# One attention block with its feed-forward part on one core: scales from norms, values by DMA transposes, and score tiles taken in pairs

## The reference

```python
c_kv = x @ w_dkv;  c_q = x @ w_dq
k_r = rope(x @ w_kr)                    # one for all heads
k = concat(k_r, c_kv @ w_uk);  q = concat(rope(c_q @ w_qr), c_q @ w_uq)
v = c_kv @ w_uv
attn = softmax(q @ k.T / sqrt(192));  out = (attn @ v) @ w_o
x = layernorm(x + out)
x = layernorm(x + (silu(x @ w1q.T) * (x @ w3q.T)) @ w2q.T)   # ternary weights
```

## Time and profile before

| | |
|---|---|
| median of three runs | 1019.66 us |
| profiled execution | 1020.77 us |
| its span | 1019.1 us |
| granted TensorE clock, mean | 0.974 of full |
| set-up | 0 to about 47 us |
| stage before the loop, batch 0 | about 47 to 112 us |
| loop, batch 0 | about 112 to 458 us |
| output, norms, feed-forward, batch 0 | about 458 to 527 us |
| loop, batch 1 | about 593 to 940 us |

### The profile page before, as it was taken

How to read it: one execution, slowest core, us unless ns; L and a number is a source line. 1 busy time by engine, 2 the same in 40 slices (tenths; PEclk the granted TensorE clock), 3 DMA queues, 4 the chain that set the end, 5 groups by cost and what they waited for, 6 DMA issues and landing times.

```text
span 1019.1 us, 17708 instructions
## 1 busy us (share of the span) xinstructions
PE 891.6 (87%) x5114; PEld 502.5 (49%) x5114; DVE 681.3 (67%) x1060; ACT 695.9 (68%) x1116; POOL 596.0 (58%) x401
## 2 busy tenths in 40 slices
PE   7888869998999999989889876999999999998985
PEld 3556534444444444448775642444444444444874
DVE  1877747777777777764458674777777777776455
ACT  2733668888888888881333466888888888887132
POOL 0008856767777767772341874776777776777134
PEclk9998979999999999999999897999999999999998
DMA  9734698887778877884510669897878877889301
GB/s 252 231 141 104 148 221 153 149 152 149 145 148 154 153 148 145 146 157 134 180 36 12 132 161 192 148 152 150 153 143 150 154 149 145 151 146 157 120 1 41
DMA packets 420800, 145.34 MB, mean 143 GB/s; under 512 B 405820, under 2 KB 413840, under 8 KB 419728
## 3 DMA queue, kind: packets, MB, share of 16 engines
q1 hardware_dynamic: 419584, 136.88, 67.5%
q10 hardware_dynamic: 592, 5.77, 1.4%
q0 software_dynamic: 576, 2.10, 0.6%
HBM read 23.85 MB, written 7.60 MB: 31 GB/s over the span
## 4 chain that ended last, share of the span: by engine, by line
PE 28%; ACT 25%; issue 20%; DVE 11%; POOL 9%; DMA 3%; ACTq 2%; SPq 1%; POOLq 0%; DVEq 0%
ACT probs L566 11%; ACT P_parts L451 8%; POOL P_parts L398 6%; PE Sb L1103 6%; DVE nmax L825 5%; PE Oa L1132 4%; ACT PT_hi L451 3%; PE Sa L1103 3%; DMA PT_dma<-P_parts 2%; ACT rden_row L451 2%; POOL g_lo L427 1%; DVE qmul L804 1%; PE Sa L1156 1%; PE Sb L1156 1%; DVE Q_parts L795 1%
## 5 line engine op out<-in xcount | busy, mean ns | idle before, releaser
L398 POOL TENSOR_TENSOR P_parts<-probs,P_parts 128x768 f16<-128x768 f32 x256 | 420.8, 1645 | 210.2 <-ACT P_parts L451 210.2
L451 ACT ACTIVATE P_parts<-probs 128x768 f16<-128x768 f32 x256 | 214.3, 838 | 17.0 <-DMA PT_dma<-P_parts 17.0
L566 ACT ACTIVATE probs<-Sa,nmax,limits 128x1024 f32<-128x1024 f32 x128 | 154.0, 1203 | 90.3 <-DVE nmax L828 90.1
L825 DVE TENSOR_REDUCE nmax<-Sb 128x1 f32<-128x1024 f32 x128 | 156.5, 1223 | 55.9 <-PE Sb L1103 55.7
L1103 PE MATMUL Sb<-K_hi,Q_parts 128*128 128x512 f16 x512 | 155.1, 385 | 43.6 <-ACT probs L566 42.8
L1103 PE MATMUL Sa<-K_hi,Q_parts 128*128 128x512 f16 x512 | 156.3, 388 | 34.8 <-ACT probs L566 34.7
L825 DVE TENSOR_REDUCE nmax<-Sa 128x1 f32<-128x1024 f32 x128 | 154.9, 1210 | 29.1 <-PE Sa L1103 29.1
L566 ACT ACTIVATE probs<-Sb,nmax,limits 128x1024 f32<-128x1024 f32 x128 | 154.3, 1205 | 1.5 <-DVE nmax L828 1.5
L1132 PE MATMUL Oa<-PT_dma,V_hi 128*64 128x512 f16 x768 | 132.4, 385 | 0.0
L1103 PEld LDWEIGHTS Sa<-K_hi,Q_parts 128*128 (+1 forms) x512 | 40.1, 99 | 118.7 <-issue 61.2
L371 POOL TENSOR_TENSOR turned<-qmul 128x1024 f32<-128x1024 f32 x16 | 40.1, 2528 | 93.5 <-DVE qmul L804 93.4
(11 more groups left out here) (300 smaller groups left out, 1536.6 us busy)
## 6 DMA issues: line engine op xcount, KB each, us to landing
Q_parts<-turned_parts SPq DMA_DIRECT2D x64, 128.0 KB, 2.4
TT<-ternary SPq DMA_DIRECT2D x2, 2304.0 KB, 9.7
Q_parts<-Q_parts SPq DMA_DIRECT2D x16, 256.0 KB, 2.9
PT_dma<-P_parts SPq DMA_TRANSPOSE x256, 3.6
ternary<-tern ACTq DMA_DIRECT2D x1, 2304.0 KB, 8.2
wo<-in_L_attn_w_o_dram SPq DMA_DIRECT2D x4, 512.0 KB, 8.6
xq<-in_L_attn_x_dram SPq DMA_DIRECT2D x2, 1024.0 KB, 12.1
wq_low<-Wq_lo ACTq DMA_DIRECT2D x1, 2048.0 KB, 12.7
```

Of the source, the lines that this page charges most:

```text
L398: nc.gpsimd.tensor_tensor(P_parts[:, n % DEEP, 1, :], probs[n % DEEP][:, KP * P:S], P_parts[:, n % DEEP, 0, :], ALU.subtract).then_inc(par ...
L451: return nc.scalar.activation(o, i, ACT.Copy, scale=scale)
L566: nc.scalar.activation(probs[n % DEEP], SS[n % 2][:, :], ACT.Exp, bias=nmax[:, n % 4:n % 4 + 1], scale=score_down, accum_out=den[:, n // 8 ...
L825: nc.vector.tensor_reduce(nmax[:, n % 4:n % 4 + 1], SS[n % 2][:, :], AX.X, ALU.max, negate=True).then_inc(row_max, 1)
```

## The change

Four things are changed together.

The scales of the fp16 parts are no longer taken from the computed keys and queries but bounded from norms: the largest sum of squares of a row of x (eight squares with accumulation on ScalarE), the largest entries of the key and query weights and the sum of squares of w_dq, with a square root by a power on GpSimd. They are known before the keys are cut, so K_hi and K_lo are cut straight from PSUM; the latent half by ScalarE and VectorE, the rotated half by GpSimd's sums. The query latent is scaled when it is cut, and later steps on queries carry no scale.

The values are no longer transposed by TensorE; SP issues two DMA transposes of the latent halves of K_hi and K_lo.

In the loop two tiles are taken at a time: TensorE computes two score tiles, then values, then the transposes of both; ScalarE makes two exponents, then the eviction PT_hi, then two casts; VectorE takes two maxima, then PT_lo, and now copies the row of sums. VectorE makes one normalising product, and GpSimd casts its high part.

The stores of the low weights pass from ScalarE's to SP's queue, and the low part of the rotary weights from VectorE to GpSimd.

```diff
 # scalar: before the loop
-                act_.wait_ge(proj_in, b * 208 + 208)
+                act_.wait_ge(w_in, b * 160 + 160)
...
+                act_.wait_ge(y_ready, b * 2 + Y0)
+                for t in range(QT):
+                    nc.scalar.activation(qmul[:, t // 4, t % 4 * D:t % 4 * D + D], xq[:, t, :], ACT.Square,
+                                         accum_out=x_sums[:, t:t + 1]).then_inc(x_sq, 1)
...
+                scaled(K_hi[64:128, :], Sa[64:128, :], k_up[64:128]).then_inc(k_lat_hi, 1)
+                scaled(cq_hi[:, :], Sb[:, :], cq_up).then_inc(cq_hid, 1)
...
 # scalar: the loop
-                    for n in range(TILES):
...
-                            exponent(t0 + n + 1, n + 1)
-                        part_high(t0 + n, n, None if first and n < DEEP else 16 * (t0 // DEEP + n // DEEP))
-                        if n % 2:
-                            transposed_high(t0 + n, n)
-                        if n in (3, 11) and not (first and n == 3):
-                            row_out(pair * 2 + (n // 8) - 1)
+                    for n in range(0, TILES, 2):
+                        ahead = not (last and n == TILES - 2)
+                        if ahead:
+                            exponent(t0 + n + 2, n + 2)
+                        if ahead:
+                            exponent(t0 + n + 3, n + 3)
+                        transposed_high(t0 + n + 1, n + 1)
+                        if ahead:
+                            for m in (n + 2, n + 3):
+                                part_high(t0 + m, m, None if first and m < DEEP else 16 * (t0 // DEEP + m // DEEP))
 # vector: before the loop
+                nc.vector.tensor_reduce(kv_most, wkv[:, :, :].rearrange("p c m -> p (c m)"), AX.X, ALU.max,
+                                        apply_absolute_value=True).then_inc(w_max, 1)
...
+                nc.vector.tensor_reduce(x_most, x_sums[:, :], AX.X, ALU.max).then_inc(x_max, 1)
+                dve.wait_ge(x_row, b + 1)
+                nc.vector.tensor_reduce(sums[0:1, 7:8], Oa[0:1, 0:P], AX.X, ALU.max).then_inc(x_top, 1)
+                dve.wait_ge(sums_ps, b + 1)
...
+                dve.wait_ge(lim_pow, b + 1)
...
+                for out_rows, in_rows, o, table in (...):
+                    nc.vector.scalar_tensor_tensor(o[out_rows, :], Sa[in_rows, :], k_up[in_rows], table[in_rows, :],
+                                                   ALU.mult, ALU.mult).then_inc(k_mul, 1)
+                nc.vector.scalar_tensor_tensor(K_lo[64:128, :], Sa[64:128, :], k_up[64:128], K_hi[64:128, :], ALU.mult,
+                                               ALU.subtract).then_inc(k_lat_lo, 1)
-                nc.vector.tensor_reduce(k_sum, Kf[:, :], AX.X, ALU.max, apply_absolute_value=True).then_inc(k_step, 1)
-                nc.vector.tensor_reduce(q_most[:, 0:1], cq_hi[:, :].bitcast(F), AX.X, ALU.max, ...)
-                nc.vector.tensor_reduce(q_most[:, 1:2], cq_s[:, :].bitcast(F), AX.X, ALU.max, ...)
...
 # vector: the loop
+                def row_out(group):
+                    dve.wait_ge(row_ps, group + 1)
+                    dve.wait_ge(out_ready, group + 1)
+                    nc.vector.tensor_copy(rden_row[:, :], Ob[:, :]).then_inc(row_ready, 1)
...
-                        if not (last and n >= TILES - 2):
+                        if not (last and n == TILES - 2):
                             maximum(t0 + n + 2, n + 2)
-                        if n % 2:
-                            transposed_low(pair * (TILES // 2) + n // 2, n)
+                            maximum(t0 + n + 3, n + 3)
+                        transposed_low(pair * (TILES // 2) + n // 2, n + 1)
+                        if n % 8 == 2 and not (first and n == 2):
+                            row_out(pair * 2 + n // 8 - 1)
 # gpsimd
+                pool.wait_ge(lim_step, b * LSTEPS + 5)
+                nc.gpsimd.tensor_tensor(pow_of, pow_in, minus_half[:, 0:2], ALU.pow).then_inc(lim_pow, 1)
+                pool.wait_ge(k_mul, b * 3 + 3)
+                nc.gpsimd.tensor_tensor(kmul[0:32, :], kmul[0:32, :], kturn[0:32, :], ALU.subtract).then_inc(k_rot, 1)
+                nc.gpsimd.tensor_tensor(kmul[32:64, :], kmul[32:64, :], kturn[32:64, :], ALU.add).then_inc(k_rot, 1)
...
+                nc.gpsimd.tensor_tensor(K_lo[0:64, :], kmul[0:64, :], K_hi[0:64, :], ALU.subtract).then_inc(k_rot_lo, 1)
...
+                    nc.gpsimd.tensor_copy(O_parts[:, pair_row, cols], QO[:, pair_row + 1, cols]).then_inc(out_hi, 1)
 # sync
+                sp.wait_ge(k_lat_hi, b + 1)
+                sp.dma_start_transpose(V_hi[:, :, :], K_hi[64:128, :]).then_inc(v_in, 16)
+                sp.wait_ge(k_lat_lo, b + 1)
+                sp.dma_start_transpose(V_lo[:, :, :], K_lo[64:128, :]).then_inc(v_in, 16)
 # tensor: before the loop
-                        if g == 1 and j == 3:
-                            turn_values()
-                            pe.wait_ge(cq_lod, b * 4 + 4)
...
 # tensor: the loop
-                    for n in range(TILES):
-                        if not (last and n >= TILES - 2):
-                            scores(t0 + n + 2, (n + 2) % TILES, p + (n + 2) // TILES)
-                        transpose_probs(t0 + n, pair * (TILES // 2) + n // 2, n, not (last and n >= TILES - 2))
+                    for n in range(0, TILES, 2):
+                        for i in range(2):
+                            if not (last and n == TILES - 2):
+                                scores(t0 + n + i + 2, (n + i + 2) % TILES, p + (n + 2) // TILES)
...
-                            if n % 2 == 1:
-                                for k in range(n % 8 - 1, n % 8 + 1):
-                                    values(pair * 2 + n // 8 - 1, 1 - n // 8, k)
+                            for k in range(n % 8, n % 8 + 2):
+                                values(pair * 2 + n // 8 - 1, 1 - n // 8, k)
+                        for i in range(2):
+                            transpose_probs(t0 + n + i, pair * (TILES // 2) + n // 2, n + i,
+                                            not (last and n == TILES - 2))
```

More of the change, by code:

```diff
@@ L26 @@
 PROB_UP_LOG = 14.0 * math.log(2.0)
-VAL_UP = 2.0 ** 8
 TILES = 4 * 4
@@ L97, in build @@
         assert AT <= K_AT
-        (K_hi, K_lo, V_hi, V_lo, vscale, limits, ffs, minus_half, nmax, den, rden, rden_wide, rden_row, stats, mv, ve,
+        (K_hi, K_lo, V_hi, V_lo, limits, x_sums, sums, scales, ffs, minus_half, nmax, den, rden, rden_wide, rden_row, stats, mv, ve,
          rstd), QO_AT = lay(
@@ L101, in build @@
             ("V_hi", [P, KT, KVR], F16), ("V_lo", [P, KT, KVR], F16),
-            ("vscale", [P, 4], F), ("limits", [P, 16], F),
+            ("limits", [P, 8], F), ("x_sums", [P, QT], F), ("sums", [P, 8], F), ("scales", [P, 16], F),
             ("ffs", [P, 8], F),
@@ L878, in _ @@
                 reciprocal(group - 1, 1)
+                row_out(group - 1)
                 def statistics(t, n):
@@ L1080, in _, with project @@
-                project((Sa[:, 0:HALF], Sa[:, HALF:S]), lambda kc: wkv[:, kc, :], kv_ps)
+                pe.wait_ge(w_in, b * 160 + 160)
+                def project(outs, lhs, n):
+                    for kc in range(KC):
+                        last = mm(outs[n], lhs(kc), xT[:, kc, n * HALF:(n + 1) * HALF],
+                                  start=(kc == 0), stop=(kc == KC - 1))
+                    return last
+                pe.wait_ge(xT_sb, b * 4 + 3)
+                project((SQ[0], SQ[1]), lambda kc: wkv[:, kc, :], 0)
@@ L1086, in turn_values @@
-                def turn_values():
-                    hold(pe, k_step, b * KSTEPS + 19)
-                    for k in range(KT):
-                        last = nc.tensor.transpose(Oa[:, k * KVR:(k + 1) * KVR], kmul[64:128, k * P:(k + 1) * P],
-                                                   ident[64:128, 64:128])
-                    last.then_inc(v_ps, 1)
+                project((SQ[2], SQ[3]), lambda kc: wdq[:, kc, :], 0)
+                pe.wait_ge(ones_ready, b + 1)
+                pe.wait_ge(w_max, b * 3 + 4)
@@ new lines, in _ @@
+                pe.wait_ge(x_top, b + 1)
+                mm(Oa[:, P:P + 1], ones_b[0:1, :], sums[0:1, 7:8], start=True, stop=True)
+                mm(Oa[:, P + 1:P + 6], ones_b[:, :], limits[:, 1:6], start=True, stop=True).then_inc(sums_ps, 1)
+                project((SQ[2], SQ[3]), lambda kc: wdq[:, kc, :], 1).then_inc(cqa_ps, 1)
+                for n in range(2):
+                    last = project((Ta[:, :], Tb[:, :]), lambda kc: wdq_b[:, kc, :, :], n)
+                last.then_inc(cqb_ps, 1)
```

262 lines of the change are left out of this document (111 added, 151 removed).

## The result

The changed kernel takes 1062.3 us in the median of 4 runs (1055.8 to 1064.8); the kernel before, on the same chip, 1019.5 us (1018.5 to 1024.8). The ratio is 1.039, 95% interval 1.034 to 1.045. The prediction said 1055, range 1036 to 1072. The profiled execution took 1064.8 us, span 1063.1.

What follows compares the result with a forecast made beforehand. No engine is full; a ring of waits between VectorE and ScalarE bounds the loop. Loops +44 us and the stage before them -9 give +35 on 1020.8, 1056, less 1.1 for the median: 1055 us, range 1036 to 1072.

Steps and rivals of the forecast that it cites:

- stage before the loop: Work ahead of the loop: removed waits and transposes against late scales and slow clock, -9 us in sum, bounds -19 to 0.
- The ring: Loop, VectorE and ScalarE: PT_lo, two maxima, exponent, PT_hi, PT_lo close at 5.30 us a step against 4.65; group 22.57.
- the walk: One batch summed from the cast awaiting the first transposing DMA to the first output matmul: 344.3 us against 322.2, +22.1.
- Copy and product: VectorE in each group's ring: row copy adds 0.60 us, one normalising product and the reciprocal 0.77.
- The late scales: Ahead of the first query term: norms must precede cutting the keys, +1.6 us in the first batch, +4.9 in the second.
- The restart of the clock: TensorE idles some 3 us ahead of the query terms and restarts at a slower clock, +1.8 us a batch.
- the removed terms: TensorE before the loop: V_lo wait, eight transposes, rotation wait and slow restart go, together 9.5 us a batch.
- The ends of the batches: Output work closing each batch: VectorE's new wait and GpSimd's cast replacing the product change nothing, +-1 us.
- (1): Loop: TensorE is the bound and the ring does not close, 19.1 us a group, 953 us in all; 7%.
- (2): Loop: the added maximum hides in VectorE's idle time, group stays at 21.07 us, 1011 us in all; 5%.
- (3): Loop: the ring of four DMA buffers makes casts wait, 1.5 us a group at a 7 us landing, 1099 us; 4%.
- (4): Stage before the loop: norms cost far more, the stage loses up to 10 us a batch, loop as forecast, 1075 us; 6%.

Runs made afterwards that it cites:

- e3: Changed kernel with VectorE's order alone altered: PT_lo of a pair put one step later, between the next step's two maxima, row copy behind the second maximum; 992.8 us.
- e4: Changed kernel with ScalarE's order alone altered: the first of the two casts to P_parts stands ahead of PT_hi, not behind it; 1150.0 us.
- e5: Changed kernel with the copy of the row of sums alone moved back to ScalarE, behind the casts of the second step; 1041.5 us.
- e7: Changed kernel with two normalising products on VectorE again and no cast on GpSimd; 1074.6 us.
- e1: Kernel before with only the loop's new order in pairs of tiles; stage before the loop, both products and row copy on ScalarE kept; 1069.9 us.
- e2: Changed kernel with the loop's order undone, one tile at a time, and the row copy back on ScalarE; the other parts stay; 991.1 us.
- e6: e2 with PT_lo alone moved behind the next maximum on VectorE; 985.3 us.
- e9: e6 with ScalarE's order alone altered: PT_hi put behind the exponent into Sb, the row copy behind the cast one tile later; 969.5 us.
- e8: Changed kernel with six further squares, output unused, ahead of the eight for the norms; 1065.4 us.
- e10: e9 with the row copy on VectorE behind an odd maximum, outside any ring; 968.2 us.

## Why the prediction was right, and where its sum was off

**The total: right, in part by errors that cancel.** The profiled execution is 44.0 longer in span, forecast +35. Loops -0.9 against the forecast, stage before the loop -3.6, ends +7.6, set-up +5.8.

**The ring: right.** Measured 5.30 a step and 22.53 a group for 5.30 and 22.57, and 344.4 us for 344.3 in batch 0 (343.2 in batch 1). The closeness is partly luck, twice. The sum as written, 4 x 5.30 + 0.77 + 0.60 - 0.10, gives 22.47 and not 22.57; with it the walk is 343.0 and +20.8 a batch. And the second cast, which the walk had behind the first at once, waited for its own DMA as well.

```profile
134.59 0.84 ACT L479 ACTIVATE P_parts<-probs 128x768 f16<-128x768 f32 x1 [5.76 <-DMA PT_dma<-P_parts]
136.07 0.84 ACT L479 ACTIVATE P_parts<-probs 128x768 f16<-128x768 f32 x1 [0.64 <-DMA PT_dma<-P_parts]
```

e3 and e4 show it as cause, not only as arithmetic that fits: one instruction taken out of the ring and one put in moved the time by -70 and +88. One of the signs to look for was mis-sized: the text said 2.7 us of idle before PT_lo, and it is 1.85; 1.50 + 1.20 + 0.62 less the maximum's own 1.22 and its 0.21 follower gives 1.9, so the sentence contradicted its own ring.

**Copy and product: right.** The copy costs 0.60 a group (e5) and a second product 0.66 (e7), each shown alone. The product and reciprocal that stayed cost 0.73 (step 6.03), for 0.77.

**The stage before the loop: right in sign, too small.** Forecast -9, measured -12.6 up to the released cast. The first score tile comes 6.7 us earlier in batch 0 (about 6 forecast) and 3.5 in batch 1 (about 3). The late scales came as worked out: cq_lo ends 19.6 us after the transposes of xT begin in both batches, against 18.0 and 14.7 before, so +1.6 and +5.0 (forecast +1.6 and +4.9). The squares were 0.40 apart, not 0.45, and ScalarE loads its table as often as before (five loads in both traces), so the doubt about a further load is settled: the Trainium skill's page "ScalarE: Activation LUTs", section "Table sets: the hidden batching unit", left it open, and no load stands between the last copy of xT and the first square here.

The restart of the clock behind the new wait was paid about as forecast, +1.8 a batch. The 18 query matmuls from the first on cq_lo took 4.25 us before in both batches, and 5.85 and 6.40 after (71.87 to 77.72, 572.67 to 579.07): +1.6 and +2.1.

```profile
55.61 3.70 PE L1072 MATMUL Sa<-xT,wkv 128*128 128x512 f32 x8 [1.44 <-ACT xT L479]
...
70.74 0.73 PE L1158 MATMUL Sa<-cq_hi,Wq_hi 128*128 128x512 f32 x2 [3.35 <-DVE K_lo L781]
71.87 1.02 PE L1158 MATMUL Sa<-cq_lo,Wq_hi 128*128 128x512 f32 x2 [0.40 <-DVE cq_lo L784]
```

In batch 0 the projections, after only 1.44 us of idle (3.21 in the earlier trace rows), ran at full rate besides, 3.70 for eight and not 5.40. That did not make the stage better than forecast, since cq_lo came when the forecast had it.

What the sum had too small are the removed terms. From the end of cq_lo to the first exponent it is 8.5 and 8.7 us less; without the clock's part 10.1 and 10.9 were removed in batches 0 and 1, where the sum has 9.5. About 0.5 of that is the small product with ones and TensorE's wait behind it (70.81 to 71.57 before), which the sum left out; in batch 1 the slow restart before also lasted 0.75 longer (568.37 to 574.31 against 88.70 to 93.89). The last 2.0 of the 12.6 lie behind the first exponent, 1.8 of them in batch 1 (24.9 us to the released cast before, 23.1 after; 23.2 and 23.0 in batch 0). Why is open. The sum without the clock term would have been -12.5 (13 in the text); that this is what was measured is chance, since the term was paid.

**The ends of the batches: wrong, and the largest miss of the sum.** Forecast "nothing, +-1", measured +2.7 and +4.9. TensorE waits 2.04 us for the last O_parts in each:

```profile
983.22 0.96 PE L1241 MATMUL Sa<-Wvo_lo,O_parts 128*128 128x256 f32 x7
986.22 0.50 PE L1241 MATMUL Sa<-Wvo_hi,O_parts 128*128 128x256 f32 x2 [2.04 <-POOL O_parts L420]
...
987.83 3.02 PE L1241 MATMUL Sb<-Wvo_hi,O_parts 128*128 128x256 f32 x14
```

GpSimd's queue at the end of batch 0:

```profile
480.10 3.28 POOL L426 TENSOR_TENSOR P_parts<-probs,P_parts 128x768 f16<-128x768 f32 x2 [2.65 <-ACT P_parts L479]
483.35 0.62 POOL L411 TENSOR_SCALAR rden_wide<-rden 128x512 f32<-128x512 f32 x1
483.91 0.61 POOL L418 CAST O_parts<-QO 128x512 fp32r<-128x512 f32 x1
484.70 1.26 POOL L420 TENSOR_TENSOR O_parts<-QO,O_parts 128x512 fp32r<-128x512 f32 x1 [0.18 <-POOL O_parts L418]
```

The prediction looked at VectorE there and had the cast merely take the place of the second product. The two last casts now stand behind both exponents and PT_hi, so GpSimd's last two low parts (3.28) begin after the first output matmul (480.10 against 478.95), and its new cast adds 0.61 and a wait. Both parts show alone: the kernel before doesn't wait for O_parts; e1, the order without the cast, waits 2.7 us in its two batches together; e2, the cast without the order, 1.7; the kernel after 4.1. e7, without the cast, still waits 1.23 of the 2.04. In batch 1 the clock fell after this wait: 14 matmuls took 3.02 for 1.85 before the wait (979.15), and from 1034.84 to 1038.04 the last products are 0.21 us apart where they are 0.12 apart before: half clock once more (0.59 granted over 1034 to 1038), 1.5 us.

**The set-up: +5.8 for a forecast of nothing, and 1.2 of it is of the change.** Both kernels have one TensorE product that waits 0.90 us for ScalarE's sum of magnitudes (at 29.29 before, 30.69 after), and it parts the set-up. From it to the transposes of xT:

```
                              us, to the transposes of xT    granted clock, 31 to 41 us
before                        17.11                          1.00
e2, e5, e6, e7                18.30, 18.32, 18.31, 18.32     1.00, 1.00, 1.00, 1.00
after, e3, e4, e9             21.51, 21.51, 21.52, 21.52     0.51, 0.63, 0.50, 0.62
```

Three runs are left out, since their clock fell for another length of time or their wait was another: e1, with the code of before, 20.01 at 0.76; e8, behind a wait of 1.46, 23.02 at 0.55; e10, behind 0.97, 20.05 at 0.90. The last two rows are the same code in this stretch and the same wait of 0.90 us. In four executions the clock goes from its full 2.4 GHz to 1.2 behind it, in four it stays, and that is 3.2 us. The kernel after, then e5 (the granted clock is the column before the last two):

```profile
31.00:41.00 10.00, 10.00 (x36) 5.48 (x36) 5.99 (x12) 3.41 (x10) 0.00 (x0) 0.51 0.85 246
```

```profile
31.00:41.00 10.00, 9.82 (x61) 6.42 (x60) 10.00 (x13) 7.72 (x21) 5.67 (x3) 1.00 0.93 260
```

The first two rows are both at full clock and differ by 1.2 us: that is the change. The low part of the rotary weights now runs on GpSimd, and VectorE's steps on the ternary weights beside it are longer: `below` 1.73 for 1.02, `w2n` 2.19 for 1.81, and in e6 one `w` 2.88 for 1.81. VectorE before and after, GpSimd after, and TensorE of e6:

```profile
39.95 1.02 DVE L691 TENSOR_SCALAR below<-w2n,ffs 128x1536 f32<-128x1536 f32 x1
41.54 1.81 DVE L695 SCALAR_TENSOR_TENSOR w2n<-w2n,ffs,below 128x1536 f32<-128x1536 f32 x1
```

```profile
45.31 1.73 DVE L702 TENSOR_SCALAR below<-w2n,ffs 128x1536 f32<-128x1536 f32 x1
47.63 2.19 DVE L706 SCALAR_TENSOR_TENSOR w2n<-w2n,ffs,below 128x1536 f32<-128x1536 f32 x1
```

```profile
43.68 8.55 POOL L380 TENSOR_TENSOR Wq_lo<-wqr,Wq_hi 128x512 fp32r<-128x512 f32 x4 [41.22 <-ACT Wq_hi L479]
```

```profile
45.60 0.66 PE L1030 MATMUL Ta<-ident,w2n 128*128 128x128 f32 x4 [1.60 <-DVE w2n L708]
```

TensorE waits 1.6 us there in e2, e5 and e7 too; no run moves the low part back alone.

The remaining 1.4 lie ahead of the product. The pairs of matmuls at L1015 (L1017 before) take 1.06 us at first and 0.59 later, the two lengths that they have in the kernel after at 0.51 and at 1.00 granted, though the profile grants 1.00 here throughout. The shorter length comes at about 21 us before, 24 after and 15 in e5. So the transposes of xT start at 52.2 in the kernel after and at 44.9 in e5: 4.1 of the 7.3 were there ahead of the product, 3.2 came behind it. These 1.4 and 3.2 differ between executions of the same code, so they are no property of a version; how much of the spread of the other runs they make isn't shown, since only one execution of each kernel has a trace.

**The rivals.** (1) and (2) are out: no PT_lo in the group starts before the second exponent has ended, and VectorE's idle 39% bought nothing. But (1)'s end state, TensorE as the bound, was there for an order that opens both rings (e9, 19.57 a group for its 19.1). The rule beside it, of the Trainium skill's page "Perfetto Trace Analysis", section "Matmul Optimizations" (matmuls back to back in batches), does not decide here: the order that has it is the slow one. (3) is out: casts waited for DMAs 4 times, 12.8 us in all, at the start of the batches. (4) is out: the stage gained.

## What to carry to other kernels

With in-order queues, write down for each repeating step the cycle of waits through all engines, add the pitches on it, and divide by the steps it spans; the longest cycle sets the time, and here shares of busy time of 60 to 70% said nothing about it. To batch two items on every engine puts the second item's whole work into the cycle; consume a hand-over one item late (PT_lo, PT_hi behind the next maximum or exponent), so that the cycle spans more steps. When a cycle is cut, compute the next longest before expecting the bound of an engine (e6 missed by 17 us for want of that).

## What the runs showed of the hardware

- The same wait of 0.90 us, at the same place in the same code, was followed by half clock for about 10 us in four executions (31 to 41 us: 0.51, 0.63, 0.50, 0.62) and by none in four others (1.00), worth 3.2 us up to the transposes of xT.
- Beside a GpSimd subtraction (L380), VectorE's steps of 1.02 and 1.81 us took 1.73 and 2.19 in the kernel after, and one of 1.81 took 2.88 in e6.
- At the start of an execution matmul pairs took 1.06 us, and 0.59 from about 15 to 24 us on, while the granted clock reads 1.00 for both.
- A square of 256 columns is 0.30 us at its pitch on ScalarE, 0.40 with the reading of the accumulator, and needs no table load beside copies. A power of 2 columns on GpSimd is 0.72 us, of 4 columns 1.02.
- The ring's waits repeat to 0.01 us: 1.85 in the kernel after, 2.58 in plain steps of e4.
